# A hybrid attention block with two expert layers on one core: three classes in the last part of the block table, and the closing loads taken in two steps

## The reference

```python
x = L0_attn_a_x                                  # 8 batches x 512 positions x 128, float32
x = x + attn_a(layernorm(x))                     # linear attention, 16 heads
x = x + ffn(layernorm(x))                        # expert layer 1
x = x + attn_b(layernorm(x))                     # fast-weight memory, 16 heads, delta rule
x = x + ffn(layernorm(x))                        # expert layer 2

def ffn(h):                                      # 8 experts, 128 -> 512 -> 128
    g = softmax(h @ Wr)
    top2_w, top2_idx = top_k(g, 2)
    top2_w = top2_w / sum(top2_w)
    hid = relu(einsum('bsh,ehf->bsef', h, W1))
    expert_out = einsum('bsef,efh->bseh', hid, W2)
    return sum(top2_w * expert_out at top2_idx)  # two experts per token
```

## Time and profile before

| | |
|---|---|
| three runs | 982.16, 985.35 (median), 987.62 us |
| the profiled execution | 982.65 us, its span 980.9 us |
| PE busy | 922.9 us, 94% |
| DVE busy | 552.7 us, 56% |
| ACT busy | 542.3 us, 55% |
| POOL busy | 371.0 us, 38% |
| mean granted clock of PE | 0.989 |

### The profile page before, as it was taken

The page is one execution under the profiler, slowest core; times in us unless marked ns, Lnnn a source line. Parts: engine busy times, 40 slices in busy tenths (PEclk is TensorE's granted clock), DMA queues, the critical chain, the costliest instruction groups (busy, mean ns, idle before and its releaser), DMA issues.

```text
span 980.9 us, 31631 instructions
## 1 busy us (share of the span) xinstructions
PE 922.9 (94%) x11919; PEld 689.2 (70%) x11919; DVE 552.7 (56%) x1966; ACT 542.3 (55%) x1082; POOL 371.0 (38%) x387
## 2 busy tenths in 40 slices
PE   7999999999999999987999889999999999998994
PEld 6446655665679999984554485568457679988994
DVE  5236465355376542206669658787777887774114
ACT  3543243334314555544776675776668575666772
POOL 2300412321333776653141012031432364766773
PEclk9999999999999999998999999999999999999998
DMA  8744224404403233205020120111023513123345
GB/s 227 224 89 88 64 53 105 109 14 97 110 23 78 75 96 99 70 24 173 3 89 2 46 89 1 46 42 60 19 63 117 193 44 76 59 75 99 97 133 205
DMA packets 80308, 82.77 MB, mean 84 GB/s; under 512 B 12207, under 2 KB 63236, under 8 KB 79648
## 3 DMA queue, kind: packets, MB, share of 16 engines
q1 hardware_dynamic: 66240, 59.61, 22.9%
q0 software_dynamic: 10176, 19.04, 6.2%
q10 hardware_dynamic: 3744, 2.10, 0.9%
HBM read 53.96 MB, written 27.64 MB: 83 GB/s over the span
## 4 chain that ended last, share of the span: by engine, by line
PE 34%; DVE 9%; issue 4%; ACT 3%; DMA 3%; SPq 1%; POOL 1%; DVEq 0%; ACTq 0%; POOLq 0%
PE b_ring L1891 8%; PE b_ring L1348 5%; PE b_ring L1359 5%; PE b_ring L1834 4%; PE b_g L1940 4%; PE b_g L1913 4%; DVE b_kq L2313 2%; PE b_ring L1955 2%; ACT early L2068 1%; ACT b_outT L2080 1%; DVE b_prod L2221 1%; DVE b_coef L2224 1%; DMA b_coef<-gram_compact 0%; PE b_s L1900 0%; SPq L1620 0%
## 5 line engine op out<-in xcount | busy, mean ns | idle before, releaser
L1891 PE MATMUL b_ring<-b_hT,b_qkT 128*128 128x512 f32 x256 | 119.9, 607 | 5.8 <-DVE b_kq L2313 4.5
L2313 DVE SCALAR_TENSOR_TENSOR b_kq<-b_exp,b_ring 128x512 f32<-128x512 f32 x128 | 83.4, 684 | 38.3 <-ACT b_exp L2048 36.4
L277 POOL DMA_INDIRECT expert_rows<-f_route_sent,f_route_place_id x64 | 62.7, 980 | 97.5 <-DVE f_route_place_id L233 50.9
L2048 ACT ACTIVATE b_exp<-b_ring 128x512 f32<-128x512 f32 x128 | 73.8, 602 | 31.5 <-PE b_ring L1891 21.6
L1891 PEld LDWEIGHTS b_ring<-b_hT,b_qkT 128*128 128x128 f32 x256 | 45.3, 189 | 61.3 <-issue 40.8
L1021 ACT ACTIVATE phik<-a_ring 128x512 f32<-128x512 f32 x64 | 38.2, 597 | 81.4 <-PE a_ring L864 81.4
L277 POOL DMA_INDIRECT expert_rows<-g_route_sent,g_route_place_id x48 | 52.9, 1103 | 74.5 <-PE b_ring L1955 28.5
L1348 PE MATMUL b_ring<-b_v,b_kq 128*128 128x128 f32 x568 | 75.4, 276 | 3.6 <-issue 2.8
L1359 PE MATMUL b_ring<-wide,b_v 128*128 x568 | 75.7, 276 | 0.5 <-issue 0.4
L1348 PE MATMUL a_ring<-phik 128*128 128x128 f32 x568 | 75.1, 275 | 0.4 <-ACT phik L1369 0.4
L1359 PE MATMUL a_wide<-wide,phiqT 128*128 x568 | 74.7, 275 | 0.0
(11 more groups left out here) (340 smaller groups left out, 1841.6 us busy)
## 6 DMA issues: line engine op xcount, KB each, us to landing
a_rn_wide<-norm_compact SPq DMA_DIRECT2D x28, 512.0 KB, 8.3
wide<-in_L_ffn_W SPq DMA_DIRECT2D x32, 256.0 KB, 5.5
a_rn_wide<-expert_rows SPq DMA_DIRECT2D x71, 65.0 KB
b_coef<-gram_compact SPq DMA_DIRECT2D x4, 1024.0 KB, 4.8
b_hT<-expert_rows SPq DMA_DIRECT2D x56, 65.0 KB
x<-in_L_attn_a_x SPq DMA_DIRECT2D x8, 256.0 KB, 4.4
early<-expert_parts SPq DMA_DIRECT2D x4, 512.0 KB, 6.0
gram_compact<-wide SPq DMA_DIRECT2D x32, 64.0 KB
```

Source lines behind the costliest of these rows:

```text
L277: pool.indirect_dma_start(self.rows, bass.IndirectOffsetOnAxis(self.place_id[:, k, n:n + 1], 0), self.sent[:, n, k, :], None).then_inc(sel ...
L1891: pe.matmul(ring[n % 4][:, :], w, hT[:, g % 2, half * 512:half * 512 + 512], start=True, stop=True)\
L2048: act.activation(exps[:, n % EXPS, :], ring[n % 4][:, :], ACT.Exp, bias=-1.0).then_inc(S["exp_ready"], 1)
L2313: dve.scalar_tensor_tensor(out=kq[:, p % 2, half:half + FOURS // 2, slot:slot + T * FOUR], in0=exps[:, n % EXPS, :].rearrange("p (a n) -> ...
```

## The change

The last phase's table has three classes: the blocks that the first six half-groups touch, those that the first seven touch besides, and the rest. For this `mark` is called a second time, at step 17, after seven half-groups have their places, and `whole` and `touched` hold two rows of counts; phase 2 keeps its two classes, written in the general form. C["below"] grows from 17x16 to 25x24. The rows of the seventh half-group are then all in the first 63 blocks (`B_NEXT`). SP, when the early pieces are stored, waits for those (rounded up to a pair of buffers, so for block 63 too) and loads pieces 0 and 1; after the last block it loads piece 2 and ACT loads piece 3. Stores and adds keep their order.

```diff
@@ -31,6 +31,7 @@
+B_NEXT = (7 * TOKENS // 4 + EXPERTS * (P - 1)) // P
@@ -293,9 +294,10 @@
 
     PARTS = 4
 
-    def __init__(self, K, C, tag, rows, scratch, bounds, ranked=()):
-
-        self.C, self.rows, self.scratch, self.bounds, self.ranked = C, rows, scratch, bounds, ranked
+    def __init__(self, K, C, tag, rows, scratch, bounds, marks=None):
+
+        self.C, self.rows, self.scratch, self.bounds = C, rows, scratch, bounds
+        self.marks = marks or {}
         self.tail_ready, self.table_step = K.sem(f"{tag}_tail_ready"), K.sem(f"{tag}_table_step")
         self.table_ready = K.sem(f"{tag}_table_ready")
         self.filler_stored = K.sem(f"{tag}_filler_stored")
@@ -306,11 +308,14 @@
         self.past_full = self.past_all[:, 0:TOKENS // P * EXPERTS].rearrange("p (b e) -> p b e", e=EXPERTS)
...
-        self.upto_all = self.area(1, (max(entries) + 1) * max(entries))[:, 0, :]
+        self.upto_all = self.inside_all
+        most_marks = max(1, max(entries) // EXPERTS - 1)
+        self.whole, self.touched = self.area(most_marks, EXPERTS), self.area(most_marks, EXPERTS)
@@ -318,7 +323,7 @@
 
     def entries(self, phase):
 
-        return 2 * EXPERTS if phase in self.ranked else EXPERTS
+        return (1 + self.marks.get(phase, 0)) * EXPERTS
 
     def by_block(self, flat, n, m):
         return flat[:, 0:n * m].rearrange("p (b e) -> p b e", e=m)
@@ -373,10 +378,10 @@
         self.then(dve, dve.tensor_reduce(out, self.past_full.rearrange("p b e -> p e b"), AX_X, ALU.add))
         self.then(dve, dve.tensor_scalar(out, out, float(P), None, ALU.mult))
 
-    def mark(self, dve):
-
-        self.rows_of(dve, self.whole, False)
-        self.rows_of(dve, self.touched, True)
+    def mark(self, dve, i):
+
+        self.rows_of(dve, self.whole[:, i, :], False)
+        self.rows_of(dve, self.touched[:, i, :], True)
 
     def count(self, dve, phase, last):
 
@@ -385,16 +390,20 @@
         self.rows_of(dve, self.n_blocks, last)
         if phase:
             self.then(dve, dve.tensor_tensor(self.n_blocks, self.n_blocks, self.used, ALU.subtract))
-        if phase in self.ranked:
-            first, second = self.n_all[:, 0:EXPERTS], self.n_all[:, EXPERTS:2 * EXPERTS]
-            self.then(dve, dve.tensor_tensor(first, self.touched if last else self.whole, self.used, ALU.subtract))
-            self.then(dve, dve.tensor_scalar(first, first, 0.0, None, ALU.max))
-            self.then(dve, dve.tensor_tensor(second, self.n_blocks, first, ALU.subtract))
+        n = self.marks.get(phase, 0)
+        if n:
+            by_class = self.by_block(self.n_all, n + 1, EXPERTS)
+            self.then(dve, dve.tensor_tensor(by_class[:, 0:n, :], (self.touched if last else self.whole)[:, 0:n, :],
+                                             self.used.unsqueeze(1).to_broadcast([P, n, EXPERTS]), ALU.subtract))
+            self.then(dve, dve.tensor_scalar(by_class[:, 0:n, :], by_class[:, 0:n, :], 0.0, None, ALU.max))
+            self.then(dve, dve.tensor_copy(by_class[:, n, :], self.n_blocks))
+            for i in range(n, 0, -1):
+                self.then(dve, dve.tensor_tensor(by_class[:, i, :], by_class[:, i, :], by_class[:, i - 1, :], ALU.subtract))
 
     def limits(self, dve, phase, lo):
 
         m = self.entries(phase)
-        n_rows = self.n_all[:, 0:m] if phase in self.ranked else self.n_blocks
+        n_rows = self.n_all[:, 0:m] if m > EXPERTS else self.n_blocks
         ends, upto = self.ends_all[:, 0:m + 1], self.by_block(self.upto_all, m + 1, m)
         self.then(dve, dve.tensor_tensor(upto, n_rows.unsqueeze(1).to_broadcast([P, m + 1, m]),
                                          self.C["below"][:, 0:m + 1, 0:m], ALU.mult))
@@ -411,8 +420,8 @@
         self.then(dve, dve.tensor_tensor(inside, past[:, :, 0:m], past[:, :, 1:m + 1], ALU.subtract))
         table = self.table_all[:, 1, 0:n]
         self.then(dve, dve.tensor_reduce(table, past[:, :, 1:m + 1], AX_X, ALU.add))
-        if phase in self.ranked:
-            self.then(dve, dve.scalar_tensor_tensor(out=table, in0=past[:, :, EXPERTS], scalar=-float(EXPERTS), in1=table,
+        for o in range(EXPERTS, m, EXPERTS):
+            self.then(dve, dve.scalar_tensor_tensor(out=table, in0=past[:, :, o], scalar=-float(EXPERTS), in1=table,
                                                     op0=ALU.mult, op1=ALU.add))
         self.then(dve, dve.tensor_scalar(table, table, float(EXPERTS - 1), None, ALU.min))
 
@@ -429,8 +438,11 @@
             for o in range(0, m, EXPERTS):
                 ins = dve.tensor_tensor(shift[:, o:o + EXPERTS], shift[:, o:o + EXPERTS], self.used, ALU.add)
             self.then(dve, ins)
-        if phase in self.ranked:
-            self.then(dve, dve.tensor_tensor(shift[:, EXPERTS:m], shift[:, EXPERTS:m], self.n_all[:, 0:EXPERTS], ALU.add))
+        by_class = self.by_block(shift, m // EXPERTS, EXPERTS)
+        for i in range(1, m // EXPERTS):
+            self.then(dve, dve.tensor_tensor(by_class[:, i:, :], by_class[:, i:, :],
+                                             self.n_all[:, (i - 1) * EXPERTS:i * EXPERTS].unsqueeze(1)
+                                             .to_broadcast([P, m // EXPERTS - i, EXPERTS]), ALU.add))
         self.then(dve, dve.tensor_tensor(start, self.C["block_rows"][:, lo:hi].unsqueeze(2).to_broadcast([P, n, m]),
                                          shift.unsqueeze(1).to_broadcast([P, n, m]), ALU.add))
         self.then(dve, dve.tensor_tensor(inside, inside, start, ALU.mult))
@@ -576,7 +588,7 @@
             dve.memset(C["expert_ids"][:, e:e + 1], float(e))
         dve.memset(C["below"][:, :, :], 0.0).then_inc(self.masks_ready, 1)
         dve.wait_ge(self.masks_ready, self.MASKS + 3)
-        for e in range(1, 2 * EXPERTS + 1):
+        for e in range(1, 3 * EXPERTS + 1):
             dve.memset(C["below"][:, e, 0:e], 1.0)
         dve.wait_ge(self.ident_step, 4)
         dve.tensor_copy(self.A["vo"][:, :, DIM], C["ident"][:, P - 1:P].to_broadcast([P, HEADS]))\
@@ -1558,7 +1570,7 @@
         router = Router(K, C, ctx, "g_route", r_bank, None, None, rows, late_sents)
         ffn = ExpertLayer(K, C, ctx, "g", 1, rows, parts, homes, (s_bank, g_bank[0]), ring[0:2], ring[2:4])
         block_table = BlockTable(K, C, "g", rows, exps[:, :, :].rearrange("p a n -> p (a n)"),
-                                 ((0, B_FULL[0]), B_FULL[0:2], B_FULL[1:3], (B_FULL[2], BLOCKS)), (2, 3))
+                                 ((0, B_FULL[0]), B_FULL[0:2], B_FULL[1:3], (B_FULL[2], BLOCKS)), {2: 1, 3: 2})
         EARLY_PART = FinalSum.EACH * FinalSum.EARLY * 2 * DIM
         early_homes = [flat[:, o:o + EARLY_PART].rearrange("p (t n) -> p t n", t=FinalSum.EACH) for flat, o in
                        ((C["early"][:, :], 0), (C["early"][:, :], EARLY_PART),
@@ -1690,8 +1702,10 @@
             sp.wait_ge(S["x_ready"], NG)
             final.load_early(sp)
             final.store_early(sp)
+            ffn.stored_before(sp, B_NEXT)
+            final.load_late(sp, (0, 1))
             ffn.stored(sp)
-            final.load_late(sp, (0, 2))
+            final.load_late(sp, (2,))
             final.store_late(sp, (0, 2))
             final.all_stored(sp)
 
@@ -2126,7 +2140,7 @@
                     if j in at:
                         routing(r, at.index(j))
             ffn.stored(act)
-            final.load_late(act, (1, 3))
+            final.load_late(act, (3,))
             final.store_late(act, (1, 3))
 
         @block.vector
@@ -2471,7 +2485,7 @@
                 elif j == 10:
                     route_statistics(7)
                 elif j == 11:
-                    block_table.mark(dve)
+                    block_table.mark(dve, 0)
                     block_table.part(dve, 1, 0)
                 elif j == 12:
                     choose(6)
@@ -2483,6 +2497,7 @@
                     route_normalize(7)
                 elif j == 17:
                     block_table.part(dve, 1, 3)
+                    block_table.mark(dve, 1)
                 elif j == 18:
                     block_table.part(dve, 2, 0)
                 elif j == 19:
@@ -2525,7 +2540,7 @@
-            "below": K.sb(ctx, "below", [P, 2 * EXPERTS + 1, 2 * EXPERTS]),
+            "below": K.sb(ctx, "below", [P, 3 * EXPERTS + 1, 3 * EXPERTS]),
```

More of the change, by code:

```diff
@@ L308, in __init__ @@
         self.past_full = self.past_all[:, 0:TOKENS // P * EXPERTS].rearrange("p (b e) -> p b e", e=EXPERTS)
-        self.inside_all = self.area(1, max((hi - lo) * n for (lo, hi), n in zip(bounds, entries)))[:, 0, :]
+        self.inside_all = self.area(1, max([(hi - lo) * n for (lo, hi), n in zip(bounds, entries)]
+                                           + [(n + 1) * n for n in entries]))[:, 0, :]
         self.table_all = self.area(2, most)
-        self.upto_all = self.area(1, (max(entries) + 1) * max(entries))[:, 0, :]
-        self.ends_all, self.capped_all, self.shift_all, self.n_all, self.n_blocks, self.used, self.whole, self.touched = (
```

(6 more changed lines are left out.)

## The result

| | median us | runs | against the kernel before, with its 95% interval |
|---|---|---|---|
| before | 984.17 | 6 | |
| changed | 988.95 | 6 | 1.0054 [1.0034, 1.0074] |
| changed, once more in a later comparison | 987.12 | 12 | 1.0038 [1.0020, 1.0056] |

What follows compares the result with a forecast made beforehand. The prediction took DVE to set PE's pace from its step 17 to its step 29, around blocks 30 to 34; +5.7 us of delay and -1.6 of tail gave +4.1 on 985.35, so 989.4 us, range 984.0 to 993.0.

Steps and rivals of the forecast that it cites:

- The second mark: On DVE before choose(7): two `rows_of` of 1.51 us each, 3.02 us added.
- DVE's sum: Added table work on DVE from before step 17 to block 34's take: 5.94 us, all passed to PE.
- The gaps of 0.78 before a take: DVE idle before four takes: taken to give nothing back; if real waits of 0.44 us, they would swallow 1.8 us.
- rival B: DVE's additions fall into time it would wait anyway; only the tail's -1.6 us is left, 983.7 us; chance 0.12.
- The stalls step by step: PE's waits: 3.92 us before `rank` of the eighth half-group, about 2.8 before block 30, 2.0 before 32, 0.9 before 34.
- Rival C: PE's clock halves in the stall before `rank`; blocks 24 and 25 +3.8 us, +1.0 at the end, 990.4 us; chance 0.10.
- The argument against C: The clock's fall was seen some 3.9 us behind the last matmul, so a stall must be that long or longer.
- The relief at block 49: PE's 0.23 us wait for block 49's rows goes, so the delay at the blocks' end is 5.7 us, not 5.94.
- The tail: After the last scatter: two pieces loaded and four adds left instead of eight, -1.6 us (-2.1 to +0.7).
- Stores 0 and 1 now follow the closing load on each queue: In the tail: these stores go ahead of the adds of pieces 2 and 3, at no cost.
- The early loads: Pieces 0 and 1, issued some 7 us before the closing loads, take 4.0 us and land by 970.
- rival D: No tail gain: early loads of pieces 0 and 1 land late or slow the last scatters; +5.7, 991.1 us; chance 0.10.

Runs made afterwards that it cites:

- e3: The changed kernel with the second mark at step 19, behind choose(7), in place of step 17: 989.84 us, 1.0045 against the kernel before.
- f4: The changed kernel without the second mark's whole count, which nothing reads: 985.24 us, 1.0004 against the kernel before; once more 986.30 us, 1.0023.
- e1: The changed kernel's table only, with the closing loads as in the kernel before: 990.57 us, 1.0064 against the kernel before.
- g2: The kernel before, keeping two classes and its closing loads, with the first mark's touched count and phase 3 moved late: 978.75 us, 0.9940.

## Why the prediction was right

- **The second mark, 3.02 us**: 1.52 us for one `rows_of` in the trace, 3.04. Right.
- **DVE's sum, 5.94 us**: T to block 35 grew by 5.60 and 5.67 us in the two profiles of the changed kernel, 6.00 with the table alone. Right, if 0.3 us high, and so is its heart, that PE pays all of it. The gaps of 0.78 before a take gave nothing back; that they might was the ground of the lower bound (4.1 us for the delay) and of rival B.
- **The stalls step by step**: before `rank` 3.92 us forecast, 3.71 and 3.93 measured; before 34, 0.9 forecast, 1.02 and 0.92. Before 30 and 32, 2.8 and 2.0 forecast, 0.2 and 1.80 measured in the first profile, 0.98 and 1.66 in the second: the clock's part, below.
- **Rival C, half right.** The clock did fall where it said, in both profiles (at 877.5 and 874.3 us), so the prediction's own sign for C came, while A's time came too. The argument against C, that a stall has to be about as long as the 3.9 us behind the last matmul, was wrong: the clock fell behind waits as short as 2.12 us. The price was too high: blocks 24 and 25 took 2.2 us more in the first profile and 1.2 in the second, not 3.8. The wait before block 30 was 2.6 and 1.8 us shorter than the forecast 2.8, so it took up the slow blocks, and the extra 1.0 us at the end didn't come. T to block 35 is within 0.4 us of e3, where the clock fell only at block 30 and block 32's wait took that up (0.34 us in place of 1.80). The Trainium skill, page "TensorE: Matmul & The Clock Gate", section "Part 1: The HAM clock gate (the "warmup" mystery)", has the array fall back to 1.2 GHz once it has sat idle. The trace agrees, with 0.50 of the full clock behind the waits of 3.71 and 3.93 us.
- **The relief at block 49, 0.23 us**: mis-sized. Block 35 to block 70 took 0.9 to 1.0 us less (67.5 to 66.5 and 66.6), and in all kernels with the delay 66.4 to 66.6, but for one profile of f4 at 67.4, which waits 0.47 us there. PE's wait in the kernel before was 0.23 us by the row, but the hidden step behind it came 0.44 late; another 0.4 lies in the last three blocks, and why is open. So of the 5.6 us, 4.7 reach the last block; the forecast was 5.7.
- **The tail, -1.63 us**: mis-sized too. The four kernels with all loads behind the last block take 11.02 us on average from last scatter to end, the ten others 9.98: -1.05. The four adds went as forecast (3.27 us to 1.67). But the first closing load lands after 3.49 us on average where it took 3.03. "Stores 0 and 1 now follow the closing load on each queue: nothing" is the step that didn't hold up: what is new in that stretch beside the loads are these stores. That they are the cause I argue from the order; no run takes them away.
- **The early loads**: they landed 4.2 and 4.3 us after issue (3.3 to 4.4 in all ten kernels), against 4.0 forecast, and DVE's last adds never waited for them; the last scatters came 0.2 us later on average with them. So rival D is out. Its bound has a slip: 964.8 + 11.1 is 975.9, not 976.1, so the upper bound is 0.2 us too high. The filling of `below` took 0.5 us more, as forecast, and the first hidden step of layer 2 came only 0.2 later in the second profile: it was covered.
- **Sum**: in the first profile the layer grew by 4.1 us (163.4 to 167.5), just the forecast, but by luck: 0.9 of it lies ahead of T, where the code is the same. T to block 35, block 35 to 70 and the tail gave 5.60 - 1.00 - 1.45 = 3.15 us; in the second profile the whole layer grew by 3.1. With the average tail it is 3.6. The terms of the forecast were off by -0.3 (the delay), -0.7 (the relief) and +0.6 us (the tail), which partly cancel. The time of 989.4 against 988.95 is closer than the forecast deserves: it was built on 985.35 us for the kernel before, which then had a median of 984.17.

## What to carry to other kernels

Before adding work to an engine that is 56% busy, look for the stretch in which it sets the pace: there each small instruction costs its whole 0.2 us, and some 12 us later the same work was free. Copy the few numbers that a later result hangs on, and work it out where the engine idles. When a wait goes, look at the next producer in the queue at once: here SP, held by one copy of eight numbers, took back 2.6 us. And where medians of different comparisons differ by more than the traces do, as f4's did, run the two side by side before explaining it.

## What the runs showed of the hardware that I had not expected

In these stretches the granted clock fell to 0.50 in or behind waits of PE of 2.12, 2.20, 2.22, 2.41, 3.32, 3.71, 3.83 (e1) and 3.93 us, and not behind the 2.41 us of the kernel before, the 2.05 of g2 ahead of T, nor 1.80. The same wait of the same code, 2.41 us, was followed by a fall in one execution and by none in another: the fall cost 1.6 us on block 30, and 0.56 us were left at block 35. That such falls are a part of the spread between executions of one kernel is likely but not shown; each kernel's trace is of one execution.
